# Reordering the late work between the score bounds and the softmax of a fused attention and mixture-of-experts kernel

## Time and profile before

| what | value |
|---|---|
| median of 3 runs | 1499.25 us (1498.46 to 1499.82) |
| the profiled execution's own time | 1497.55 us |
| its span, first to last instruction | 1495.8 us |
| mean granted TensorE clock | 0.964 of full speed |
| busy share of PE, DVE, ACT, POOL | 91%, 74%, 56%, 36% |

### The profile page before, as it was taken

One profiled execution on the slowest core, in us unless ns is written; L12 is line 12 of the kernel. 1 busy time (PEld: TensorE's weight loads), 2 busy tenths in 40 slices (PEclk: granted clock), 3 DMA queues, 4 the chain that ended last, 5 costly groups with the idle time before them and its releaser, 6 DMA issues.

```text
span 1495.8 us, 29484 instructions
## 1 busy us (share of the span) xinstructions
PE 1364.3 (91%) x11220; PEld 754.5 (50%) x11220; DVE 1107.3 (74%) x2746; ACT 840.4 (56%) x1266; POOL 538.3 (36%) x638
## 2 busy tenths in 40 slices
PE   5687999999998999989999999989999899999697
PEld 3322565436654466435655366543664347543364
DVE  6993689857897588966889477985879668895534
ACT  5407763395635866277643967348662776429321
POOL 4203442254323542244422543235432453225143
PEclk8757999999999999999999999999999999999899
DMA  6001021200212011211222003210122101220031
GB/s 248 8 7 16 30 73 64 51 30 21 82 66 49 15 59 57 71 30 30 65 70 52 16 30 87 64 37 30 51 66 64 37 16 59 71 57 16 14 110 61
DMA packets 52209, 77.78 MB, mean 52 GB/s; under 512 B 6322, under 2 KB 26724, under 8 KB 51812
## 3 DMA queue, kind: packets, MB, share of 16 engines
q1 hardware_dynamic: 52068, 75.89, 17.3%
HBM read 66.95 MB, written 8.65 MB: 51 GB/s over the span
## 4 chain that ended last, share of the span: by engine, by line
PE 45%; DVE 25%; ACT 13%; issue 7%; POOL 4%; DVEq 3%; DMA 2%; SPq 1%; POOLq 0%
PE PS L572 10%; PE PS L560 8%; PE PS L715 7%; ACT UQ L991 7%; DVE CM L1327 6%; POOL hp L1047 4%; PE PS L489 4%; PE PS L506 3%; DVE hr L1140 3%; ACT UK L991 2%; ACT hp L851 2%; DVE CM L1249 2%; PE PS L777 2%; PE PS L725 2%; PE PS L397 2%
## 5 line engine op out<-in xcount | busy, mean ns | idle before, releaser
L1047 POOL TENSOR_TENSOR hp<-hr,hp 128x512 f16<-128x512 f32 (+1 forms) x200 | 241.0, 1205 | 593.3 <-ACT hp L851 561.4
L1327 DVE TENSOR_REDUCE CM<-PS 128x32 f32<-128x1024 f32 x320 | 378.5, 1220 | 35.1 <-PE PS L489 31.1
L572 PE MATMUL PS<-W,hp 128*128 128x256 f16 (+1 forms) x2400 | 314.1, 274 | 21.5 <-POOL hp L1047 19.5
L560 PE MATMUL PS<-x1T,W 128*128 128x512 f16 (+1 forms) x1200 | 307.5, 382 | 0.0
L572 PEld LDWEIGHTS PS<-W,hp 128*128 128x128 f16 (+1 forms) x2400 | 214.3, 98 | 109.6 <-POOL hp L1047 47.0
L851 ACT ACTIVATE hp<-hr 128x512 f16<-128x512 f32 (+1 forms) x178 | 112.7, 633 | 233.8 <-DVE hr L1140 218.9
L842 ACT ACTIVATE hr<-PS,CF 128x512 f32<-128x512 f32 (+1 forms) x200 | 136.9, 684 | 185.8 <-PE PS L560 180.5
L1140 DVE TENSOR_TENSOR hr<-hr,gB 128x512 f32<-128x512 f32 x176 | 128.2, 728 | 76.1 <-ACT hr L842 71.7
L560 PEld LDWEIGHTS PS<-x1T,W 128*128 128x128 f16 (+1 forms) x1200 | 107.4, 99 | 109.4 <-issue 30.0
L991 ACT ACTIVATE UK<-PS 128x1024 f32<-128x1024 f32 x160 | 152.9, 1037 | 10.7 <-PE PS L506 10.2
L991 ACT ACTIVATE UQ<-PS 128x1024 f32<-128x1024 f32 x160 | 150.9, 1041 | 3.4 <-PE PS L506 1.9
(11 more groups left out here) (151 smaller groups left out, 1883.1 us busy)
## 6 DMA issues: line engine op xcount, KB each, us to landing
gB<-gates SPq DMA_DIRECT2D x64, 256.0 KB, 3.3
gB<-gates SPq DMA_DIRECT2D x32, 224.0 KB, 3.0
gB<-gates SPq DMA_DIRECT2D x32, 192.0 KB, 3.0
gB<-gates SPq DMA_DIRECT2D x32, 160.0 KB, 2.5
xT<-in_xT SPq DMA_DIRECT2D x8, 512.0 KB, 3.7
qET<-rows SPq DMA_DIRECT2D x16, 256.0 KB, 5.1
v<-in_x SPq DMA_DIRECT2D x8, 512.0 KB, 4.1
gB<-gates SPq DMA_DIRECT2D x32, 128.0 KB, 2.9
```

The source lines that it names most:

```text
L560: mm = pe.matmul(PS[0:w, BK_H[c % 2], :], W1[:, a, k, bass.ds(f0, w)], x1T[:, e, k, :], start=(n == 0), stop=(n == 5))
L572: mm = pe.matmul(PS[:, BK_Y + j // 2, (j % 2) * D:(j % 2 + 1) * D], hp[0:w, slot, a, j * P:(j + 1) * P], W2[0:w, e, bass.ds(c, 1), :].rear ...
L1047: nc.gpsimd.tensor_tensor(hp[0:w, slot, 1, :], hr[0:w, slot, :], hp[0:w, slot, 0, :], ALU.subtract).then_inc(pool_hp, 1)
L1327: nc.vector.tensor_reduce(dst, src, AX.X, ALU.max).then_inc(dve_cm, 1)
```

## The change

It reorders instructions on PE, ACT and DVE in turns 1 to 7 (in turn 0 only the gate's products and the transposes trade places). No instruction is added or taken away, and no buffer changes.

- DVE: `gated(22)` goes from behind the reduction of j = 1 to behind that of j = 2; `gated(23)` from behind j = 2 to behind j = 3; `gated(24)` stays last.
- PE: the output gate's products go behind the four transposes of `negm` and `up(24)`; `down(23)` goes from ahead of the key units to between units 1 and 2 of group 0, `down(24)` from there to between units 3 and 4.
- ACT: both maxima go ahead of `high(23)` and `relu(24)`; `output_gate(1)` goes ahead of `high(24)`.

```diff
@@ PE @@
+                for j in range(NT):
+                    if m is not None and j == 2:
+                        late_up(NC - 1)
+                    pe.wait_ge(dve_bias, b * NT + j + 1)
+                    mm = pe.transpose(PS[0:H, 2 + j // 3, j * P:(j + 1) * P], negm[:, j, :], ident)
+                    if j >= 2:
+                        mm.then_inc(pe_neg, 1)
                 pe.wait_ge(dve_cm, (b + 1) * TU + RING)
                 for j in (0, 2, 1, 3):
...
-                for j in range(NT):
...
                 if m is not None:
                     late_down(NC - 3)
-                    late_down(NC - 2)
...
-                for d in range(2):
+                for d in range(NU):
                     unit(0, 0, d)
-                if m is not None:
-                    late_down(NC - 1)
-                for d in range(2, NU):
-                    unit(0, 0, d)
+                    if m is not None and d in (1, 3):
+                        late_down(NC - 2 + d // 2)
@@ ACT @@
                     high(m, NC - 3, (NC - 3) % 2)
+                maxima(0)
+                maxima(1)
+                if m is not None:
                     high(m, NC - 2, (NC - 2) % 2)
                     relu(m, NC - 1, (NC - 1) % 2)
-                maxima(0)
-                maxima(1)
                 output_gate(0)
+                output_gate(1)
                 if m is not None:
                     high(m, NC - 1, (NC - 1) % 2)
-                output_gate(1)
@@ DVE @@
-                    if m is not None and j >= 1:
-                        gated(m, C_BIAS[0] + j - 1, (C_BIAS[0] + j - 1) % 2)
+                    if m is not None and j == 2:
+                        gated(m, C_BIAS[0], C_BIAS[0] % 2)
+                if m is not None:
+                    for c in range(C_BIAS[0] + 1, C_BIAS[1]):
+                        gated(m, c, c % 2)
                 if m is not None:
                     finish(m)
```

## The result

| | before | after |
|---|---|---|
| median | 1499.53 (1498.46 to 1499.97, 4 runs) | 1514.82 (1513.53 to 1515.51, 4 runs) |
| profiled execution, its span | 1497.55, 1495.8 | 1515.51, 1513.7 |
| mean granted clock | 0.964 | 0.956 |

The ratio is 1.0098, 95% interval 1.0083 to 1.0113: slower by 15.3 us, where 11.8 were forecast. The two profiled executions lie 18.0 apart.

A forecast was written before the change was run, and what follows sets the result against it. ACT's back-to-back exponentials set a turn, by the first one's start and any late one. 5 x 1.5 + 2 x 0.6 = 8.7, plus 3.2 for clock falls, on 1497.55 gave 1509.45, median 1511; range 1501.5 to 1518.

The forecast's parts named there:

- the front: Start of a turn on DVE, ACT and PE: first exponential 1.0 earlier, limited by `high(24)` and no longer the DMA.
- group 0: First group's units on PE: `down(24)` later, `finish` at 476.81 instead of 475.62; 0.1 of the 1.0 left at group 1.
- the copy decides: `copy_outputs(0)` right behind `finish` on DVE: made late, it delays group 2's fourth exponential; a turn 1.5 longer.
- The rival that the start wins: Third group can do without `copy_outputs(0)` for another 1.5, so the 1.0 at the start is kept: 1492; 7%.
- the slack: The chain through `finish` and `copy_outputs(0)` to group 2's fourth exponential has some 0.3 to spare, no more.
- the crossing: Last four passes of `finish` on DVE meet POOL's three selects: 0.7 more taken, if they meet by halves.
- 0.9 without POOL: Lower end of a turn's delay: group 2's fourth exponential 0.9 late from the later `finish`, POOL's selects left out.
- bound for alternating: If DVE and POOL alternate, each of the four `finish` passes waits for a select: at most 1.9 more.
- the new gap: PE idles 1.5 ahead of group 2's dense work; clock falls in 2 of 7 turns at 1.6 each, 3.2 more.
- PE, front: Gate's products moved behind the last transpose, and `down(22)`, lie under the wait for the DMA: no cost.
- The rival that the clock falls in every turn behind the gap: Clock falls after the new PE gap in all seven turns: 8.7 + 11.2 = 19.9 more, 1519; 10%.

The follow-up runs named there:

- x5: Changed kernel with 8 + 5 idle matmuls on PE at the front only (8 ahead of the last transpose, 5 behind `down(22)`): 1510.12, ratio 1.0071.
- x1: Changed kernel with its PE placement of `down(23)` and `down(24)` undone, DVE and ACT still in the new order: 1502.11, ratio 1.0022.
- x3: Changed kernel with `copy_outputs(0)` ahead of the last four passes of `finish` on DVE instead of behind them: 1499.69, ratio 1.0001.
- x8: x5 with group 1's four POOL selects cut to one column per head, leaving the causal rule out of most of group 1: 1497.32, ratio 0.9994.
- y3: Kernel before the change, with `copy_outputs(0)` ahead of the last four passes of `finish`: 1498.33, ratio 0.9987.
- x2: Kernel before the change, with only the PE placement of `down(23)` and `down(24)` changed: 1516.51, ratio 1.0113.
- x4: Changed kernel with 16 idle matmuls on PE just ahead of `to_tokens(0)` in group 2: 1508.79, ratio 1.0070.
- y2: x3 with `down(24)` between units 2 and 3 of group 0 instead of 3 and 4: 1496.39, ratio 0.9977.
- y5: y2 with the 8 + 5 idle matmuls of x5 at the front: 1494.40, ratio 0.9958.
- y6: x3 with the 8 + 5 idle matmuls of x5 at the front: 1497.86, ratio 0.9986.

## Why the prediction was right, and which term was mis-sized

**Right: the front.** First exponential 1.0 earlier (9.79 for 10.77), limited by `high(24)`. The chain names the key units ahead of it, but by these it could have started at 654.10 (0.43 behind their start, as in the kernel before); it starts 0.54 behind that of `high(24)` in turn 3 and in every turn of x5. x1 and x3 keep this order on DVE and ACT and come out 2.4 above the kernel before and level with it, so the front is the smaller part of the cost.

**Right: group 0.** `finish` 1.22 later (1.19 said), the two holes 0.40 and 0.51, 0.9 together, as much as the prediction had given back of the 1.0 by then; first exponential of group 1 unmoved (15.48 for 15.46).

**Right: the copy decides.** It stood right behind `finish` and pushed the fourth exponential of group 2. x3 removes it and nothing else, and the loss goes. The rival that the start wins needed 1.5 of slack. Where the copy binds, in x5 and x8, the fourth exponential starts 2.74 behind it, and in the kernel before 3.07 behind it (22.76 - 19.69): the slack was 0.33, 0.3 said. y3 agrees: with the copy earlier in the kernel before, turns with an unfallen clock end where they did (48.53 in turn 5 of either). Stage 1.46 longer without a fall, 1.5 forecast, and by its parts: `finish` 1.22 later, 0.55 more from there to the copy (7.84 - 7.29, the crossing, put at 0.7), less the slack of 0.33, is 1.44. By x8 the crossing's whole price is 1.3, so the split of the 1.5 into 0.9 without POOL and the rest with it leaned on a kernel before that already paid for crossings.

The Trainium skill (SBUF — State Buffer, Who interferes with whom) says that a VectorE operation in a two-port mode and a GpSimd one block each other for a whole instruction, by order of issue; it lists `tensor_scalar`, which the four passes are, among those that can run in such a mode. The trace agrees for VectorE: four passes grow from 1.38 to 2.37 beside three selects, and are back at 1.38 when the selects are small; in turn 3 the last three passes end at 664.60, 665.23 and 665.87, each 0.15 behind the end of a select. So the two alternate, and each of these passes loses about 0.33 (0.99 in all), not a whole select: the prediction's bound for alternating, 1.9, was too high.

**Mis-sized: the clock.** The term "the new gap" took two falls at 1.6, 3.2 in all. The price was right, 1.5 (x5), the number wasn't (four), and the place was incomplete. The stage ends of turns 1 to 7 in the profiled execution sum to 360.9; unfallen (50.0 a turn, 49.8 in turn 4, 50.3 in turn 5) they would be 350.1, so falls took 10.8: 5.9 behind the gap in four turns, 4.9 at the front in five. The front falls appear nowhere in the prediction: its *PE, front* put the moved products at no cost. The gate's products, small ones of 8 rows, the wait for the last transpose (1.16 idle) and that for the DMA had come to lie together, and I had only asked whether they cost time on the path, not what they do to the clock. x1, with the downs back, still has three front falls, and x2, with the downs alone, none, so they come with the new order at the front; which of its moves brings them wasn't isolated. That the time lay in the stated range with these 4.9 missing is luck in this part. In sum: 7 x 1.46 - 1.7 (the two falls of before) + 10.8 = 19.3 in the turns, less 1.6 behind them (104.5 against 106.1), by which the spans should differ by 17.7; they differ by 17.9. The medians differ by 15.3.

The rival that the clock falls in every turn behind the gap had 10%. It was four of seven in the kernel after and two of seven in x5 and x2 with the same gap; x4 shows a fall in all seven turns, but at the front. The Trainium skill (TensorE: Matmul & The Clock Gate, HAM oscillation) has a fall in a loop at "Every single K-tile", but each of those waits about 3 to 5 us for a DMA; the waits of PE in this gap are shorter (0.87 and 1.38 in turn 3), so no run here shows that case. What decides for a given turn whether the clock falls is left open: the turns run the same instructions, and no run isolated it.

## What to carry to other kernels

When work is pushed later to let something start sooner, follow it to its last reader in the same queue: here the 1.0 won at the first exponential was paid back in one group, and then 1.5 lost because an unrelated copy stood behind the late work on DVE. Before moving the late work back, try moving the innocent instruction ahead of it. Here that only brought the time back to that of the kernel before (x3, 1.0001); a gain came with `down(24)` one unit earlier as well (y2, 0.9977) and the idle matmuls (y5, 0.9958). And count each new light stretch of PE, on the path or not, as a chance of a slower stretch behind it.

## What the hardware showed that I had not expected

The clock fell at the front, in stretches where PE was busy for 2.24 of 3.40 (turn 1 of the kernel after), not only after near idleness (1.15 of 3.40 in turn 3). Thirteen idle matmuls, about 1.4 of PE time in waits that were there anyway, kept it up at the front in every turn of x5 to x8, y5 and y6. And the untouched end of the program took 104.5 at a granted clock of 0.92 and 108.9 at one of 0.86, a difference larger than what several edits of this study moved.
